# Transposed attention outputs moved into the next step, between inner and across-chunk outputs

## The reference, cut to what matters

```python
num = jnp.einsum('bhti,bhtij->bhtj', Q, S)          # S: running sum of K (x) V
den = jnp.maximum(jnp.einsum('bhti,bhti->bht', Q, z), EPS_DEN)[..., None]
out = (num / den).transpose(0, 2, 1, 3).reshape(b, t, H * DV)
return out @ Wo
```

## Time and profile before

| | us |
|---|---|
| median of 3 runs (823.12 to 825.85) | 823.36 |
| the profiled execution | 825.21 |
| its span, first to last instruction | 823.4 |
| PE busy | 708.9 (86%) |
| PE weight loads busy | 588.0 (71%) |
| DVE busy | 540.0 (66%) |
| ACT busy | 433.1 (53%) |
| POOL busy | 246.5 (30%) |

### The profile page before, as it was taken

One profiled execution on the slowest core, in us unless ns is written; L12 is line 12 of the kernel. 1 busy time (PEld: TensorE's weight loads), 2 busy tenths in 40 slices (PEclk: granted clock), 3 DMA queues, 4 the chain that ended last, 5 costly groups with the idle time before them and its releaser, 6 DMA issues.

```text
span 823.4 us, 24414 instructions
## 1 busy us (share of the span) xinstructions
PE 708.9 (86%) x9317; PEld 588.0 (71%) x9318; DVE 540.0 (66%) x1571; ACT 433.1 (53%) x832; POOL 246.5 (30%) x286
## 2 busy tenths in 40 slices
PE   3889999999999999999999999887798968899900
PEld 2678878878878877887887888676687856778800
DVE  5666777868777877786787687776354553444445
ACT  5545584665556567457556655633353523344424
POOL 3000031134043034113313213302544353233356
PEclk9999999999999999999999999999999989899965
DMA  6700000010010001001101000002111223312155
GB/s 199 231 28 2 2 27 28 16 41 28 9 43 18 16 15 43 25 16 41 27 9 34 2 15 18 25 18 67 50 43 40 67 56 111 102 51 55 48 156 159
DMA packets 47286, 40.84 MB, mean 50 GB/s; under 512 B 5424, under 2 KB 42032, under 8 KB 47056
## 3 DMA queue, kind: packets, MB, share of 16 engines
q1 hardware_dynamic: 36368, 26.52, 11.4%
q0 software_dynamic: 4544, 9.73, 3.6%
q10 hardware_dynamic: 6272, 3.16, 1.4%
HBM read 24.93 MB, written 14.45 MB: 48 GB/s over the span
## 4 chain that ended last, share of the span: by engine, by line
PE 58%; DVE 13%; ACT 12%; issue 8%; DMA 2%; POOL 2%; SPq 2%; ACTq 2%; another core or an unknown queue 1%; DVEq 1%; POOLq 0%
PE banks_sc L515 7%; PE banks_o L675 5%; PE banks_o L496 5%; PE bank_u L400 4%; PE banks_o L506 4%; DVE work L1119 3%; PE bank_u L489 3%; PE bank_q L388 2%; PE bank_q L390 2%; ACT work L828 2%; PE bank_q L389 2%; ACT work L822 2%; ACT work L820 2%; ACT work L826 2%; PE bank_k L388 2%
## 5 line engine op out<-in xcount | busy, mean ns | idle before, releaser
L1464 POOL DMA_INDIRECT routed_rows<-routed,slot x64 | 63.2, 988 | 160.5 <-PE banks_sc L515 130.7
L1542 POOL DMA_INDIRECT expert_results<-work x72 | 69.5, 966 | 123.1 <-ACT work L924 115.5
L758 ACT ACTIVATE work<-bank_u 128x512 f32<-128x512 f32 x64 | 38.3, 599 | 124.6 <-PE bank_u L400 124.6
L675 PE MATMUL banks_o<-w,work 128*128 x576 | 79.4, 282 | 7.9 <-DVE work L1346 3.8
L1135 DVE TENSOR_TENSOR work<-banks_sc,causal 128x1024 f32<-128x1024 f32 x64 | 78.0, 1218 | 4.5 <-PE banks_sc L515 2.4
L675 PEld LDWEIGHTS banks_o<-w,work 128*128 128x128 f32 x576 | 72.0, 196 | 10.3 <-issue 9.9
L515 PE MATMUL banks_sc<-work 64*64 64x128 f32 x2048 | 72.2, 277 | 7.3 <-ACT v_aug L758 1.7
L1119 DVE SCALAR_TENSOR_TENSOR work<-bank_q,work 128x512 f32<-128x512 f32 x64 | 43.8, 684 | 45.9 <-ACT work L822 39.4
L496 PE MATMUL banks_o<-v_aug,work 128*64 128x65 f32 x2048 | 70.7, 221 | 0.0
L515 PEld LDWEIGHTS banks_sc<-work 64*64 64x64 f32 x2048 | 58.1, 134 | 13.5 <-issue 11.3
L496 PEld LDWEIGHTS banks_o<-v_aug,work 128*64 128x64 f32 x2048 | 65.3, 138 | 0.0
(11 more groups left out here) (266 smaller groups left out, 1811.7 us busy)
## 6 DMA issues: line engine op xcount, KB each, us to landing
work<-routed_rows SPq DMA_DIRECT2D x74, 66.0 KB
work<-in_L_attn_x SPq DMA_DIRECT2D x16, 256.0 KB
v_aug<-expert_results SPq DMA_DIRECT2D x8, 512.0 KB, 4.6
stage<-in_L_ffn_w SPq DMA_DIRECT2D x8, 256.0 KB, 2.7
b_rows<-in_L_ffn_b SPq DMA_DIRECT2D x1, 2048.0 KB, 15.2
moe_input<-routed SPq DMA_DIRECT2D x8, 256.0 KB
work<-moe_input ACTq DMA_DIRECT2D x8, 256.0 KB, 4.8
out<-work SPq DMA_DIRECT2D x8, 256.0 KB, 2.3
```

Of the source, the lines that this page charges most:

```text
L675: mm = pe.matmul(Y[:, 0:D], hTe[n % 2][:, blk(f)], w2[:, bass.ds(e * F + f * D, D)], start=(f == 0), stop=(f == NF - 1))
L1464: pool.indirect_dma_start(rows_d, bass.IndirectOffsetOnAxis(slot[:, k, c:c + 1], 0), routed[:, c, k, :], None).then_inc(sct, 16)
L1542: pool.indirect_dma_start(res_d, bass.IndirectOffsetOnAxis(xg[k][:, D:D + 1].bitcast(U32), 0), yw[k], None).then_inc(res_st[k], 16)
```

## The change

The four transposes `otr(g-2)` leave the end of step g-1 and stand in step g, between `columns(g-1)` and `across(g-1)`, for all p except 4; the waits for `q_phi` and `k_phi` of g move ahead of them. What would be transposed for step 4 is still done at the end of step 3. The transposes write bank B, in step 3 bank A, and for step 4 and the very last pair bank F as before. ScalarE's `ot_high(g-2)` moves from the end of its step g-1 to the start of its step g. VectorE's order is unchanged; only the bank that `ot_low` reads is another. The wait for `ot_lo` ahead of `scores` is left only in step 4, and stands ahead of the next writer of bank A or B instead.

```diff
+        def ot_bank(g):
+            p = (g + 2) % PAIRS
+            return bkF if p == 4 or g == B * PAIRS - 1 else bkA if p == 3 else bkB
...
-                turn(bkF, lambda c: on[:, c, :]).then_inc(ot_mm, 1)
+                turn(ot_bank(g), lambda c: on[:, c, :]).then_inc(ot_mm, 1)
...
                     columns(g - 1)
-                    across(g - 1)
-
                 pe.wait_ge(q_phi, g + 1)
                 pe.wait_ge(k_phi, g + 1)
+                if g > 1 and p != 4:
+                    otr(g - 2)
+                if g > 0:
+                    across(g - 1)
+
                 pe.wait_ge(v_sb, min(CH + g, 2 * CH * B))
-                if g > 1:
+                if g > 1 and p == 4:
                     pe.wait_ge(ot_lo, g - 1)
...
+                    if p in (5, 6):
+                        pe.wait_ge(ot_lo, g - 1)
...
+                    if p == 3 and g > 1:
+                        pe.wait_ge(ot_lo, g - 1)
                     q_proj(npar, np_)
...
+                    if p not in (3, 4) and g > 1:
+                        pe.wait_ge(ot_lo, g - 1)
                     k_proj(npar, np_)
...
-                if g > 0:
+                if g > 0 and p == 3:
                     otr(g - 1)
...
             columns(g_last)
+            otr(g_last - 1)
             across(g_last)
...
# ScalarE
+                if g > 1 and p != 4:
+                    ot_high(g - 2)
                 if not first:
...
-                if g > 0:
+                if g > 0 and p == 3:
                     ot_high(g - 1)
...
+            ot_high(B * PAIRS - 2)
             rows_hi(0, 0)
```

More of the change, by code:

```diff
@@ L806, in ot_high @@
                 act.wait_ge(ot_mm, g + 1)
-                copy(oT[0][:, :], bkF[:, :]).then_inc(ot_hi, 1)
+                copy(oT[0][:, :], ot_bank(g)[:, :]).then_inc(ot_hi, 1)
             def ktok_copy(g):
@@ L1130, in ot_low @@
                 dve.wait_ge(ot_hi, g + 1)
-                low(oT[1][:, :], bkF[:, :], oT[0][:, :]).then_inc(ot_lo, 1)
+                low(oT[1][:, :], ot_bank(g)[:, :], oT[0][:, :]).then_inc(ot_lo, 1)
             def mask(g):
```

## The result

The changed kernel takes 859.05 us, the median of 6 runs (855.18 to 862.21), against 824.48 us, the median of the kernel before beside it: a ratio of 1.042 [1.039, 1.045]. The forecast was 861.0, slower, in a range of 836 to 876. One of the six runs of the kernel before took 1140.22 us; the ratio leaves it out and is that of the five others, which lie between 823.08 and 825.85. The profiled execution took 862.21 us and its span is 860.4 us, 37.0 us more than before. Lines of the changed kernel stand 5 to 18 further down: `columns` L494, inner outputs L501, across outputs L511, scores L520, transposes L405, projections L393 to L395, v's L417 to L419, ScalarE's rounding copy L773, `ot_low` L1009, mask L1153, phis L1137.

A forecast was written before the change was run, and what follows sets the result against it. TensorE fills its steps almost without a gap, and whatever delays `ot_low` delays step 7. Step terms sum to 5.47 us a batch, 37.6 in all, which against 823.36 gives 861.0; range 836 to 876.

The forecast's parts named there:

- Steps 2, 6 and 7: Attention steps ending later behind a late `ot_low`: +1.07 (k's phi), +0.84 (`norm3`, `x3_t`), +1.55 us (mask, `top2`, `ranks`).
- Step 4: Attention step whose end loses its transposes before `ffn2`, with q's phi ready sooner: 0.18 us shorter.
- Rival 1: Only TensorE's stream counts, VectorE's delay fits its idle time: 1.6 us a batch, 10 in all, 833; chance 0.14.
- the gains at the ends of steps 0, 4 and 5: Transposes removed at step ends: 0.43 us where `columns` follows (0 and 5), 0.18 in step 4, elsewhere 0.
- Rival 2: Faster: transposes fall into a TensorE gap; steps 0, 4 and 5 gain some 0.4 each, -9 us, 814; chance 0.06.
- Rivals 3 and 4: 3: nothing moves, within 2 us, 823, chance 0.06. 4: VectorE bounds each step, some 64 us, 887, chance 0.08.
- TensorE's insertion: Four transposes between inner and across outputs: across outputs 0.68 us later (0.21 to 0.9), all after the scores 0.47 later.
- step 1: Attention step p=1: q's projection, its phi and `y_t` 0.47 us late, a phi wait replacing the transposes; +0.47.
- Steps 0 and 5: Step 0: v's projection waits for the mask, +0.70 us; step 5: `k_proj` waits for `residual2`, +0.68.
- The neighbour rows: Nearest measured tile-shape changes, 64x64 to 128x128 and 128x128 to 128x64, each 0.17 us idle; taken twice for the inserted transposes.
- step 3: Step keeping its end transposes; starved instruction issue inside L506 (1.8 us) may swallow the added ones: 0 to 0.68, taken 0.34.
- the hand-over: Behind the last pair, before the experts: adds 1.4 us; the experts behind it shift as a whole.

The follow-up runs named there:

- spare transposes: Kernel before plus four unread identity transposes between inner and across outputs (none in step 4), real ones still at the step's end: 816.31 us, ratio 1.010.
- the kernel with steps 1 and 6: Kernel before with the transposes moved in steps 1 and 6 alone, through bank B, `norm3` of step 6 ahead of `ot_low`: 805.34 us, ratio 0.9953.

## Why the prediction was right

**The mechanism held.** The prediction said that `ot_low`, near the head of VectorE's queue, would come to stand behind a round trip inside the step: predicted T + 2.85, measured 2.76; `den` 3.45 and 3.37; mask 4.5 and 4.40. The two experiments on VectorE show that this is the cause, one from each side: VectorE alone made late gives 1.054, and its pieces put ahead of the wait bring 1.049 down to 1.018. Steps 2, 6 and 7 came within 0.1 us of the forecast (0.97, 0.79, 1.48 for 1.07, 0.84, 1.55), and each ended in the wait named. Step 4 came out at -0.18, as predicted.

**Rivals.** Rival 1 (TensorE's stream alone) has its measured price in the spare transposes, 1.55 us a batch, where the changed kernel has 4.46 and 5.64. That the rival forecast 1.6 is chance: its sum counted the gains at the ends of steps 0, 4 and 5, which the spare transposes leave out. With these gains (0.44, 0.18 and 0.43 us) TensorE's stream alone gives about 0.5. Rival 2 asked for transposes that cost less than 0.63 us in steps followed by `columns`; it is 0.58, so the gain is there, but only at the ends of steps 0 and 5 and with VectorE out of the way, as in the kernel with steps 1 and 6. Rivals 3 and 4 fall: step lengths grow, and the plain steps hide the late mask.

**Mis-sized: TensorE's insertion.** It was taken as 0.68 us to the across outputs and 0.47 to the scores, with 0.17 us of idle on either side. Measured are 0.58 and 0.29 (T + 2.02 and 2.37). The gap on entering from 128x64 is 0.07, not 0.17; and the scores' loads start 0.35 us behind the across outputs' instead of 0.64. The idle 0.20 ahead of the scores is part of that, the rest was in the spacing. So the plain step 1 cost 0.26 instead of 0.47. Steps 0 and 5 came out 0.21 and 0.23 below forecast for another reason: their waits end 0.09 sooner (T + 6.55 for 6.64, and T + 6.27 for 6.36), as the transposes start 0.10 sooner, and behind a wait the second weight load of a projection follows at 0.11 us, not at 0.23 as in the spacing that was used. The neighbour rows were right about leaving 128x128 and wrong about entering it. The Trainium skill (TensorEngine Tiling (Array Packing), Key Properties) has every change of mode drain TensorE. The trace shows idle time on the way from 128x128 to 64x64 (0.17 us) and next to none from 128x64 to 128x128 (0.07, the same as between the two narrow shapes).

**Missed: step 3.** The prediction said that a starved stretch "may swallow" the insertion and took half of the insertion's 0.68 us as its price. The term was wrong in kind: what waits there is `h2_t`, for `norm2`, behind `ot_low`. It is worth 1.37 us a batch where these gaps are absent, on the second chip and in batch 1 of the first (1.38); in the later batches of the first chip the stretch with the gaps took it in but for 0.20. Those gaps sum to 1.29 us, not to 1.8.

**Mis-sized: the hand-over**, 5.9 us instead of 1.4. From the last T to the first expert tile it is 4.9 us on the first chip and 4.6 on the second, and all but 0.3 of the 4.6 goes with the place of the last-but-one pair's transposes; the 1 us and more behind it is open.

**The two errors cancelled.** The attention was forecast 36.2 us longer and came out 31.2 longer from first to last T (536.2 to 567.4 us); the rest was 5.9 instead of 1.4. The sum of 37.6 met 37.0 partly by luck. On the second chip, without the gaps in step 3, the first to last T grew by 37.2 us (526.6 to 563.8), near the 36.2 of the forecast, but by 5.64 us in a batch where it had 5.47, with step 3 a whole microsecond over its term and TensorE's insertion under it. Inside the 31.2 are some 2.4 us from stretches at the lower clock in steps 0 of two batches, which are 1.8 and 1.6 us longer where others are 0.5; no term stood for them.

## What to carry to other kernels

When an operation near the head of an in-order queue reads something that was produced a step earlier, it finds it ready; move the producer into the same step, and the whole round trip (here 0.69 us to the copy, 0.60 the copy, 1.4 us of idle on VectorE) is paid at that place. Move the consumer back with it, behind pieces that don't need it, or leave the producer alone. Cost such a move by asking, step by step, which late piece has a waiter: four moved transposes cost TensorE 0.25 us a step and the kernel up to 1.5 in one step, and they pay only in the two steps where the next work could start at once and nothing waited for the late pieces.

## What the runs showed of the hardware

- The idle time of the weight loads at a change of tile shape differs by direction, at full clock and between f32 tiles: 0.17 us from 128x128 to 64x64, from 64x64 to 128x128 and from 128x128 to 128x64, but 0.07 from 128x64 to 128x128 and to 64x64, on both chips.
- Gaps in TensorE's stream for which the profile shows no releaser can differ from chip to chip and within one run: on the first chip the same program's step 3 takes 10.54 us in batch 1, 12.13 to 12.18 in batches 2 to 6 and 11.75 in batch 7, on the second 10.54 to 10.57 in all seven (9.2 us less), while the other steps of a batch in mid-run agree to 0.02 us. The kernel before takes 15 us less on the second chip; the rest of that lies behind the attention and was not looked into.
- The granted clock fell to its lower level at the end of the attention in the changed kernel, where TensorE had stood idle for 3.7 and 0.8 us just before, and one such stretch lasted 13.7 us. But in the kernel before it fell there on the second chip behind 1.43 and 0.81 us of idle time, and on the first it did not behind 1.43 and 0.92. So these runs don't give the cause of a fall, nor show that the change brought it about.
